# The causal mask of transposed attention scores: from products on TensorE to a select on GpSimd

## The reference

```python
Q = x @ Wq + bq; K = x @ Wk + bk; V = x @ Wv + bv
Q, K = _rope_pair(Q, K)                       # 16 heads of 8 columns, n = 1024
scores = jnp.einsum('bhqd,bhkd->bhqk', Q, K)
causal = jnp.triu(jnp.ones((n, n), dtype=bool), k=1)
scores = jnp.where(causal, -jnp.inf, scores)
attn = jax.nn.softmax(scores / jnp.sqrt(jnp.float32(HEAD_DIM)), axis=-1)
ctx = jnp.einsum('bhqk,bhkd->bhqd', attn, V)
return ctx.transpose(0, 2, 1, 3).reshape(bsz, n, d) @ Wo + bo
```

## Time and profile before

| | |
|---|---|
| time, median of 3 runs | 1520.08 us (1519.51 to 1529.19) |
| the profiled execution, time | 1533.84 us |
| its span | 1532.0 us |
| TensorE busy in the span | 1244.8 us (81%) |
| VectorE busy | 968.8 us (63%) |
| ScalarE busy | 805.9 us (53%) |
| GpSimd busy | 696.5 us (45%) |
| attention's units, by the timeline | 330.3 to 628.4 us |

### The profile page before, as it was taken

One profiled execution on the slowest core, in us unless ns is written; L12 is line 12 of the kernel. 1 busy time (PEld: TensorE's weight loads), 2 busy tenths in 40 slices (PEclk: granted clock), 3 DMA queues, 4 the chain that ended last, 5 costly groups with the idle time before them and its releaser, 6 DMA issues.

```text
span 1532.0 us, 28182 instructions
## 1 busy us (share of the span) xinstructions
PE 1244.8 (81%) x10384; PEld 788.8 (51%) x10384; DVE 968.8 (63%) x2178; ACT 805.9 (53%) x1580; POOL 696.5 (45%) x586
## 2 busy tenths in 40 slices
PE   3889997689999998688999889834778888876894
PEld 2667675323333333366777656612656666653653
DVE  4896666676777775589666731437478888873312
ACT  4667675236666667666767421316555656520321
POOL 2766555661221100176655626115278777862211
PEclk9989999658999999898999975956688879876677
DMA  6200000000000000011000012111411111011012
GB/s 193 69 28 0 1 1 1 1 1 1 1 1 1 1 1 1 14 42 55 1 0 1 1 50 60 33 24 53 121 41 40 37 39 38 28 60 40 29 51 67
DMA packets 57324, 47.08 MB, mean 31 GB/s; under 512 B 20955, under 2 KB 50403, under 8 KB 56293
## 3 DMA queue, kind: packets, MB, share of 16 engines
q1 hardware_dynamic: 55141, 41.08, 9.0%
q0 software_dynamic: 2048, 4.20, 0.9%
HBM read 31.06 MB, written 14.20 MB: 30 GB/s over the span
## 4 chain that ended last, share of the span: by engine, by line
PE 47%; DVE 19%; issue 15%; ACT 12%; POOL 3%; SPq 2%; DMA 2%; another core or an unknown queue 0%; POOLq 0%; DVEq 0%; ACTq 0%
PE ps L709 12%; PE ps L892 5%; PE ps L859 4%; PE ps L1004 4%; DVE arena L1870 3%; PE ps L810 3%; ACT hr L1171 2%; PE ps L976 2%; DVE arena L1943 2%; ACT arena L1171 2%; DVE xn L1651 2%; PE ps L794 2%; PE ps L875 2%; ACT arena L1282 2%; PE ps L808 2%
## 5 line engine op out<-in xcount | busy, mean ns | idle before, releaser
L1546 POOL TENSOR_TENSOR arena<-arena 128x512 f32<-128x512 f32 x126 | 214.9, 1725 | 93.2 <-ACT arena L1282 39.7
L709 PE MATMUL ps<-xp,wup 128*128 128x512 f32 x768 | 209.0, 418 | 14.0 <-ACT hr L1171 9.6
L1570 POOL TENSOR_TENSOR hr<-arena,hr 128x512 fp32r<-128x512 f32 x128 | 172.5, 1353 | 85.3 <-ACT hr L1171 85.3
L1282 ACT ACTIVATE arena<-ps 128x512 f32<-128x512 f32 x256 | 143.5, 597 | 114.0 <-PE ps L976 108.2
L709 PE MATMUL ps<-hr,wdn 128*128 128x512 f32 x768 | 199.8, 410 | 1.4 <-DVE hr L1803 1.1
L1171 ACT ACTIVATE arena<-ps 128x512 f32<-128x512 f32 x256 | 162.4, 635 | 61.7 <-PE ps L709 61.4
L1237 ACT ACTIVATE arena<-ps 128x1024 f32<-128x1024 f32 (+1 forms) x192 | 150.6, 812 | 69.7 <-PE ps L878 37.3
L1803 DVE TENSOR_TENSOR hr<-arena,hr 128x512 fp32r<-128x512 f32 x128 | 127.1, 1005 | 86.7 <-ACT hr L1171 85.7
L709 PEld LDWEIGHTS ps<-xp,wup 128*128 128x128 f32 x768 | 148.3, 200 | 63.6 <-POOL wup L1557 15.7
L1943 DVE TENSOR_TENSOR arena<-arena,ps 128x1024 f32<-128x1024 f32 x189 | 154.5, 857 | 21.5 <-PE ps L989 21.1
L1171 ACT ACTIVATE hr<-ps 128x512 fp32r<-128x512 f32 x256 | 164.5, 642 | 0.0
(11 more groups left out here) (241 smaller groups left out, 2152.6 us busy)
## 6 DMA issues: line engine op xcount, KB each, us to landing
arena<-up_dram SPq DMA_DIRECT2D x16, 256.0 KB, 2.9
arena<-dn_dram SPq DMA_DIRECT2D x16, 256.0 KB, 3.2
ys_rows<-arena SPq DMA_DIRECT2D x8, 320.0 KB, 2.5
arena<-up_dram SPq DMA_DIRECT2D x2, 1024.0 KB
arena<-dn_dram SPq DMA_DIRECT2D x2, 1024.0 KB
arena<-xs_rows SPq DMA_DIRECT2D x4, 512.0 KB, 4.5
b_parts<-arena SPq DMA_DIRECT2D x1, 1536.0 KB, 5.2
dt_parts<-arena SPq DMA_DIRECT2D x1, 1536.0 KB, 6.1
```

What stands on the lines that cost most here:

```text
L709: mm = e.matmul(out, left(a), right(b), start=(first and n == 0), stop=(last and n == 2))
L1282: e.activation(to, ps[:, 4 + n % 2, :].rearrange("p (d m t) -> p t m d", d=DBK, t=TU), ACT.Exp, scale=-1.0).then_inc(SC["decay_ready"], 1)
L1546: e.tensor_tensor(hsf[t % 3][:, cols], decayf[u % 2][:, t4 * W + cols.start:t4 * W + cols.stop], hsf[(t - 1) % 3][:, cols], ALU.mult).then ...
L1570: e.tensor_tensor(hr[:, ex % 2, 1, fc, :], hid[:, ex % 2, fc, :], hr[:, ex % 2, 0, fc, :], ALU.subtract).then_inc(MX["rest_pool"], 1)
```

## The change

The mask products of the transposed scores and their matrix `hide_k` go. ScalarE exponentiates unmasked scores in the diagonal tiles. GpSimd then writes zeros into the first 128 columns of all four heads, where the key's partition is larger than the query's column (`affine_select`), in place, and the value product of a diagonal step waits for that (`cut`) and no longer for the exponentials. GpSimd's work of a unit is put in this order: cut 0, place v, cuts 1 to 3, split, cuts 8 to 11. It now runs `pool_unit` in all 8 units.

```diff
-        hide_k = sb("hide_k", [P, P], BF16)
...
+        NDI = sum(j // 4 == half for half, j in steps)
...
                     e.wait_ge(AT["exp_done"], 2 * NST * v + n + 1)
-                    diag = j // 4 == half
                     for h in range(2):
                         rows = slice(h * HR, (h + 1) * HR)
                         mm = e.matmul(ps[:, 2 + 2 * pair + h, 0:w], kT[v % 3][rows, pair, j * P:(j + 1) * P],
-                                      qm[rows, vp, pair, half * 512 + q0:half * 512 + 512], start=True, stop=not diag)
-                    for h in range(2 if diag else 0):
-                        mm = e.matmul(ps[:, 2 + 2 * pair + h, 0:P], identb[:], hide_k[:], start=False, stop=True)
+                                      qm[rows, vp, pair, half * 512 + q0:half * 512 + 512], start=True, stop=True)
                     mm.then_inc(AT["st_done"], 1)
                 elif what == "pv":
                     half, j = steps[n]
                     q0, w = span(n)
-                    e.wait_ge(AT["exp_done"], 2 * NST * v + 2 * n + 4)
+                    if j // 4 == half:
+                        e.wait_ge(AT["cut"], NDI * v + n - half * 4 + 1)
+                    else:
+                        e.wait_ge(AT["exp_done"], 2 * NST * v + 2 * n + 4)
...
-            e.wait_ge(AT["masks_ready"], 1)
...
-            e.copy(hide_k[:], maskf[:, 1, :]).then_inc(AT["masks_ready"], 1)
...
-            def pool_unit(u, par, at, more=True):
-
-                e.wait_ge(AT["pv_done"], NST * u + 2)
-                e.sem_inc(waited, 1)
-                place_v(u + 1, 1 - par, at(1))
-                if more:
+            def cut(u, m):
+
+                half, j = steps[m]
+                assert j // 4 == half
+                e.wait_ge(AT["exp_done"], 2 * NST * u + 2 * m + 4)
+                probs_now = probT[:, m % 2, :, 0:P]
+                e.affine_select(probs_now, probs_now, [[0, HG], [1, P]], ALU.is_ge, 0.0, base=0,
+                                channel_multiplier=-1).then_inc(AT["cut"], 1)
+
+            def pool_unit(u, par, at):
+
+                cut(u, 0)
+                if u + 1 < NU:
+                    e.wait_ge(AT["pv_done"], NST * u + 2)
+                    e.sem_inc(waited, 1)
+                    place_v(u + 1, 1 - par, at(1))
+                for m in (1, 2, 3):
+                    cut(u, m)
+                if u + 2 < NU:
                     e.wait_ge(AT["returned"], NRE * u + NRE)
                     e.wait_ge(AT["turned"], NTU * u + NTU)
                     e.sem_inc(waited, 1)
                     split(u + 2, par, at(2))
+                for m in range(NST - 4, NST):
+                    cut(u, m)
...
-                    if not first and not (isinstance(u, int) and u >= NU - 1):
-                        pool_unit(u, par, at, not (isinstance(u, int) and u == NU - 2))
+                    if not first and u < NU:
+                        pool_unit(u, par, at)
```

More of the change, by code:

```diff
@@ L379, in build @@
             "qkv_done", "qkv_copied", "qkv_taken", "rotated",
-            "masks_ready", "causal_ready", "pads_ready", "parts", "unit_split", "v_placed", "turned", "turned_copied", "returned",
+            "causal_ready", "pads_ready", "parts", "unit_split", "v_placed", "turned", "turned_copied", "returned",
             "returned_copied", "s_done", "max_done", "max_part", "negmax_ready",
-            "st_done", "exp_done", "pv_done", "o_copied", "o_turned", "o_summed", "o_normed", "ctxT_turned", "ctxT_ready",
+            "st_done", "exp_done", "cut", "pv_done", "o_copied", "o_turned", "o_summed", "o_normed", "ctxT_turned", "ctxT_ready",
             "proj_done", "proj_added")}
```

## The result

The changed kernel takes 1517.69 us (median of 20 runs, 1509.84 to 1522.36), the kernel before, run beside it, 1526.38 us (20 runs, 1513.68 to 1530.93). The ratio is 0.9949 with a 95% interval of 0.9932 to 0.9966: 0.5% faster, 7.8 us (5.2 to 10.4 by the interval; the two medians are 8.7 us apart). The forecast was 0.4% and 1514.3 us in a range of 1505 to 1528. The profiled execution has a span of 1515.5 us.

What follows compares the result with a forecast made beforehand. TensorE, the fullest engine, was taken to bind a unit's last stretch, taking turns with VectorE in the first. Units 0 to 5 -5.4, unit 6 -0.6, unit 0 -1.3, unit 7 +1.5: -5.8 us, 1514.3 us, range 1505 to 1528.

Steps and rivals of the forecast that it cites:

- the first stretch: Steps 0 to 5 of a unit: TensorE and VectorE take turns, so removed mask products were counted as gaining nothing.
- the unknown: Length of GpSimd's new select, taken as 1.0 us, between 0.79 and 1.73; 14 us for each 1 us longer.
- Steps 8 and 9: Diagonal steps where TensorE is the bound: removed pairs give 0.33 and 0.22 us a step, 1.1 us a unit.
- Product 10: Value product in step 11: waits for the select, costs 0.2 us, and takes what steps 10 and 11 would give.
- product 0: Value product in step 1: could start at 453.43 us with the select, starts at 453.46 now; nothing lost or gained.
- Unit 0: First unit, steps 0 to 3 at 1.2 GHz with TensorE the bound: removed products gain some 1.3 us there.
- Unit 6: Unit without turns, its end hanging on VectorE's last maximum: half the usual gain, -0.6 us, chosen.
- Unit 7: Last unit, bound by ScalarE and TensorE's order; nothing covers the select at its end: loss 1.5 us.
- The clock: Rival in unit 0: less early TensorE work, so the clock rises later and undoes the gain; 1520 us, chance 0.06.
- The select at more than one pass: Slower rival on GpSimd: select priced at two passes, 2.58 us, giving +31 us, 1551 us; chance 0.10.
- TensorE as the bound throughout: Much faster rival: every removed pair in all units gives 0.33 us, 42 us together, 1478 us; chance 0.06.
- The splitting: Rival on GpSimd: splitting for the unit after next ends too late for the first turn; 2 us, 1516 us, chance 0.04.

Runs made afterwards that it cites:

- cut_twice: Changed kernel with a second select of the same size, on a spare tile, ahead of each select: 36.76 us a unit at full clock, against 35.63.
- late_new: Kernel before with only steps 8 to 11 of each unit cut on GpSimd, steps 0 to 3 keeping mask products: 36.26 us a unit, ratio 1.0052.
- early_new: Kernel before with only steps 0 to 3 of each unit cut on GpSimd, steps 8 to 11 keeping mask products: 37.03 us a unit, ratio 1.0009.
- the second pair: Both kernels, unaltered, profiled once more: attention 295.5 us in the kernel before, 286.1 us in the changed one; ratio 0.9989.
- no_mask: Changed kernel without selects, so without any causal mask, value products waiting for exponentials alone: 35.23 us a unit at full clock, 1484.39 us in a single execution.
- zero128: Changed kernel, select kept, with the old 128-row mask products put back, adding zeros: 37.67 us a unit, 1508.58 us in a single execution.
- mask64: Kernel before with the mask kept on TensorE, as two 64-row products for each head, no select: 35.52 us a unit, ratio 0.9906.
- both: Changed kernel with the select split by pair of heads and two q-returning products moved ahead of value product 10: 35.16 us a unit.
- after_fill: Changed kernel with 30 useless 128-row products at three places of unit 7 where TensorE waits for ScalarE: unit 7 34.90 us, against 34.62.

## Why the prediction was right, and where it was off

**The time.** 0.4% was forecast, 0.5% measured, by the mechanism named. That the two lie so close is in part luck. Attention was forecast 5.8 us shorter and was 12.3 and 9.4 us shorter in the two pairs of profiles: the select had been taken too dear and the first stretch at nothing, while the loss at the end of attention had been taken too small.

**The select (the unknown).** Taken as 1.0 us, bounded below by a cast of 786 ns; it takes 0.64 us. A row of the same size is no floor for another operation. The Trainium skill (GPSIMD Engine Reference, Elementwise — side-by-side cycle accounting) has 768 ns for the tightest one-input loop of 512 elements and 12 cycles an element for branching on data; the select stays below both, and the measurement decides. The handoffs were taken as 0.20 + 0.1 us from the earlier trace rows; they are 0.07 + 0.05. The 0.20 was read from an instruction that stands behind a wait on TensorE and an extra semaphore increment; which of the two made it longer was not tried. So a value product follows its exponential by 0.76 us and not 1.3. By the prediction's own 14 us for each 1 us that makes 7.6 us more, -13.4 in all, and the two pairs of profiles show -12.3 and -9.4 in attention. The slope held in `cut_twice` (1.8 us a unit for each 1 us, against 2) from 0.76 to 1.40 us of wait, which is the stretch that this sum uses.

**Steps 8 and 9.** 1.1 us a unit were forecast. `late_new` gives 1.41 for steps 8 to 11, and the timeline shows the forecast's two terms (0.22 and 0.32 us in step 8).

**Product 10.** Forecast to cost 0.2 us, it gives some 0.3: it waits for GpSimd, but less than the removed products gave.

**The first stretch.** Forecast at nothing, measured 0.64 us (`early_new`). The step said that product 0 is held by the select at just the old time, and that was a coincidence of the 1.3 us; it also said that VectorE binds the stretch, and only from product 0 on did the removed pairs give nothing (17.65 us both times).

**Unit 0.** Forecast 2.2 us (1.3 + 0.9), measured 3.2 and 3.5. The step said that it runs at 1.2 GHz through steps 0 to 3; in the second pair it does so for its first 8 to 10 us only.

**Unit 6.** Forecast 0.6, measured 0.2, and 0.8 us lost in the second pair, at a clock of 0.95. The step said that its end hangs on VectorE's last maximum. `no_mask` shows that the products did stand in the way there: without them and without the select the unit is 1.0 us shorter. It is the wait for GpSimd that takes most of this back, and the step had no such term.

**Unit 7 and the clock.** Forecast +1.5 us by the select, measured +1.2 and +3.4. `zero128`, with products and select, has some +1.2 at full clock. But the step had the removed products give nothing at the end, and by `no_mask` they give some 2.3 us in the unit; so the near hit of the first pair is the difference of two terms, each larger than forecast. The clock was a rival, but placed in unit 0; there it rose no later than in the kernel before, pair by pair. What paid was the end: in the changed kernel the granted clock fell in unit 6 or at its end and again in unit 7, in both profiles; in the kernel before once in unit 7 in one profile, and not at all in the other. Those falls are already in the 12.3 and 9.4 us of attention. The 7.8 us of the time have an interval of 5.2 to 10.4 us, which holds the 9.4; outside attention the first pair of profiles differs by 4.2 us and the second by 0.3, so nothing was given back there in either. Why the time gains less than the first pair's 12.3 us is not shown: two profiles of each kernel are few.

**The rivals.** The select at more than one pass is out (0.64 us). TensorE as the bound throughout is out (`early_new`). The splitting never came late: it ended at 458.5 us, 3.4 ahead of the first turn.

## What to carry to other kernels

A short product that contracts over more rows than its neighbours costs far more than its columns: 0.31 against 0.05 us for the same pair. Before such work is moved to another engine, see whether it can be cut to the neighbours' rows; here that gave 35.52 us a unit against 35.63, and without a new wait (0.9906 against 0.9949 in the time, with intervals that touch). Where an operation is priced by its nearest rows, keep the range open below as well as above. And a kernel with less work on TensorE can lose some of the gain to the clock: with the mask products of 128 rows units 1 to 5 had no fall in three executions, and of the variants without them, or with half of them, five had some (`no_mask`, `cut_twice`, `mask64`, `both`, `early_new`), as had `after_fill`, and the others none. Look at the granted clock of each stretch, not at its mean over the program.

## What the runs showed of the hardware

- GpSimd's select of 512 float32 elements a partition took 637 ns by the median of 64 in one execution and 634 in the other (single ones up to 956), of 256 elements 406 ns (`both`); a cast of 512 took 787 ns in the changed kernel.
- Where it was what they waited for, GpSimd started 0.07 us after ScalarE's instruction had ended, TensorE 0.05 us after GpSimd's.
- 32 products of 128 rows and 128 columns a unit cost 1.94 us more than 32 of 64 rows and 128 columns between products of 64 rows.
- In `no_mask` the granted clock fell to 1.2 GHz for some 3 us in every other one of units that were otherwise alike, after 14 us in which TensorE had waited at most 0.56 us at a time; in units 1 to 5 of the changed kernel it fell in neither of two executions, once in a third (`after_fill`), which has filling in unit 7. What decides it is open.
